# Attention queries and keys in two fp32r parts over 48 rows, two heads per tile at rows 0 and 64

## What is computed

```python
q_half = q_lat @ Wq_up.T + bq_up
q = concatenate([q_half, apply_rotary(q_half, cos, sin)], -1)
k_half = kv_lat @ Wk_up.T + bk_up
k = concatenate([k_half, apply_rotary(k_half, cos, sin)], -1)
v = kv_lat @ Wv_up.T + bv_up
scores = einsum('bhqd,bhkd->bhqk', q, k) / sqrt(16)
out = einsum('bhqk,bhkd->bhqd', softmax(scores), v)
h = out @ Wo.T + bo
```

## Time and profile before

| | us |
|---|---|
| median of 3 runs | 823.37 |
| lowest and highest | 819.76, 823.95 |
| span of the profiled execution | 817.9 |
| start of the first score's maximum | 36.59 |
| end of the last score's maximum | 132.1 |
| start of the output projection's transposes | 150.00 |

### The profile page before, as it was taken

The page is one execution under the profiler, slowest core; times in us unless marked ns, Lnnn a source line. Parts: engine busy times, 40 slices in busy tenths (PEclk is TensorE's granted clock), DMA queues, the critical chain, the costliest instruction groups (busy, mean ns, idle before and its releaser), DMA issues. The chain is left out here.

```text
span 817.9 us, 11514 instructions
## 1 busy us (share of the span) xinstructions
PE 752.8 (92%) x3994; PEld 553.5 (68%) x4004; DVE 541.3 (66%) x1323; ACT 266.5 (33%) x421; POOL 221.1 (27%) x190
## 2 busy tenths in 40 slices
PE   5989999999999999999999498998957999999995
PEld 4422332477888888887456387777743899999995
DVE  4798996467555555555799999999577354334346
ACT  2555678453343434343571111121230100000000
POOL 4542000022232323231030000876002254434321
PEclk9999999999999999999999799999987999999997
DMA  8594000101111111140122405200014999999972
GB/s 297 172 200 94 3 2 2 59 21 38 39 50 46 55 41 54 42 155 1 40 77 81 190 1 171 62 1 1 1 52 154 320 346 346 342 340 347 342 260 97
DMA packets 39333, 101.04 MB, mean 124 GB/s; under 512 B 5374, under 2 KB 19894, under 8 KB 38326
## 3 DMA queue, kind: packets, MB, share of 16 engines
q1 hardware_dynamic: 35334, 91.06, 34.4%
q0 software_dynamic: 3504, 8.98, 2.9%
q10 hardware_dynamic: 448, 0.39, 0.2%
HBM read 84.17 MB, written 16.44 MB: 123 GB/s over the span
## 5 line engine op out<-in xcount | busy, mean ns | idle before, releaser
L1365 PE MATMUL psum<-xr,wr 128*128 128x512 f32 x600 | 145.6, 393 | 1.0 <-DVE arena L2017 1.0
L1365 PEld LDWEIGHTS psum<-xr,wr 128*128 128x128 f32 x600 | 113.6, 190 | 25.3 <-issue 1.7
L735 POOL TENSOR_TENSOR wr<-ring,wr 128x512 fp32r<-128x512 f32 (+1 forms) x50 | 54.9, 1119 | 237.5 <-ACT wr L914 145.9
L1680 PEld LDWEIGHTS psum<-arena 128*128 128x128 f32 x700 | 83.5, 192 | 3.3 <-issue 1.5
L1680 PE MATMUL psum<-arena 128*128 128x128 f32 x700 | 83.9, 275 | 1.1 <-ACT arena L1118 0.6
L1690 PE MATMUL psum<-arena 128*128 128x256 f32 x350 | 81.3, 379 | 0.0
L2480 DVE TENSOR_SCALAR arena<-psum,arena 128x256 f32<-128x256 f32 x35 | 16.9, 484 | 94.1 <-PE psum L1690 94.1
L1376 PE MATMUL psum<-hr,wr 128*128 128x512 f32 x300 | 76.6, 391 | 0.9 <-DVE hr L1954 0.9
L1865 DVE TENSOR_REDUCE small<-psum 128x1 f32<-128x512 f32 x112 | 71.1, 685 | 9.0 <-PE psum L1241 8.3
L1980 DVE TENSOR_TENSOR hid<-hid,psum 128x512 f32<-128x512 f32 x50 | 34.4, 687 | 58.6 <-ACT hid L920 58.4
L889 ACT ACTIVATE arena<-psum 128x1024 f32<-128x1024 f32 x64 | 63.1, 1023 | 27.9 <-PE psum L1251 27.2
(11 more groups left out here) (391 smaller groups left out, 1219.9 us busy)
## 6 DMA issues: line engine op xcount, KB each, us to landing
arena<-in_w1u SPq DMA_DIRECT2D x35, 642.5 KB
arena<-in_w1d SPq DMA_DIRECT2D x35, 640.0 KB
ring<-in_w SPq DMA_DIRECT2D x25, 384.0 KB, 3.1
z_scratch<-w_a SPq DMA_DIRECT2D x4, 768.0 KB, 7.1
arena<-z_scratch SPq DMA_DIRECT2D x8, 384.0 KB, 5.9
arena<-part_scratch SPq DMA_DIRECT2D x9, 256.0 KB, 7.6
qkv_scratch<-arena SPq DMA_DIRECT2D x4, 512.0 KB, 2.7
arena<-qkv_scratch SPq DMA_DIRECT2D x4, 512.0 KB, 4.0
```

The lines of the kernel that those rows point to most:

```text
L735: pool.tensor_tensor(wr0[:, k, LO, part], ring0[:, k, part], wr0[:, k, HI, part], ALU.subtract).then_inc(s["w0_lo"], 1)
L1365: ins = pe.matmul(bank[2 * b + m][:, :], wr0[:, k, w, lo:lo + P], xr[:, x, f, half(b)], start=(f == 0 and (w, x) == PARTS[0]), stop=(f == ...
L1680: ins = pe.matmul(bank[2 + r % 2 * 3 + k // 2][:, tile(k % 2)], wup1[:, r % NW, lo:lo + P], xgT[:, r % 2, f, :], start=(f == 0), stop=(f = ...
```

## The change

- Queries and keys are held in two parts, high and low, as fp32r; three pairings (HI HI, HI LO, LO HI) make 48 rows instead of 96. A row tile holds two heads side by side and two at partition 0 and 64 (`head_rows`); the maxima's rows are 48, 49 and 112, 113.
- For tiles 0 and 2, ACT makes the high part straight from PSUM, DVE the low part in one instruction; for the rotated tiles ACT and POOL do one each. Four writes per pair and batch replace six, of 4-byte words. Rows are loaded in eight issues per tile instead of seven. Rows of ones are filled once and copied by DMA.
- Every group's maxima, the first too, go through DRAM, in two loads for the two row halves. SP's loop over the groups also issues the rows of tiles 2 and 3.
- PE: the value projection comes first, then 28 scores (`FIRST`) ahead of the loop, with the gate rows' chunks, their transposes and warming matmuls between them; in the loop each step alternates `scores_t` of one half with a score of the other, two scores per step throughout. The maxima of a group are transposed four scores after its last.

The diff, cut to its core:

```diff
 HG = 4
 NG = NH // HG * B
 Q = P // HG
-KP = (0, 1, 2, 0, 1, 0)
-QP = (0, 0, 0, 1, 1, 2)
-KRUN = ((0, 3), (3, 5), (5, 6))
-QRUN = ((0, 1), (1, 2), (2, 4), (4, 6))
+HI, LO = 0, 1
+PARTS = ((HI, HI), (HI, LO), (LO, HI))
+KP = (HI, LO, HI)
+QP = (HI, HI, LO)
+KRUN = ((0, 2), (2, 3))
+QRUN = ((0, 1), (1, 3))
 KR = HD * len(KP)
+HROW = P // 2
+HP = HG // 2
 DK, DV = 8, 16
 E0, K0, I0 = 16, 6, 176
...
-AHEAD = 4
-HI, LO = 0, 1
-PARTS = ((HI, HI), (HI, LO), (LO, HI))
+FIRST = HG * TB + 12
+MAX_LAG = 4

...
+        def head_of(n):
+
+            return n // 8 % HP, 1 - n % 2, n // 2 % TB
+
...
+            first = FIRST + 2 * (2 * TB * g + p)
+            return range(first, min(first + 2, NG * HG * TB))
+
+        def maxima_after(n):
+
+            g, over = divmod(n + 1 - MAX_LAG, HG * TB)
+            return g - 1 if over == 0 and g > 0 else None
...
         def k_rows(eng, t, own, name):
-            for r, end in KRUN:
-                eng.dma_start(Kt[t][r * HD:end * HD, :, own], piece_rows(1, t, r, end)[:, :, own])\
-                   .then_inc(s[name], 16)
+            for jb in range(2):
+                for r, end in KRUN:
+                    eng.dma_start(head_rows(Kt[t], jb, r * HD, end * HD)[:, :, own].bitcast(F32),
+                                  piece_rows(1, t, r, end, jb)[:, :, own]).then_inc(s[name], 16)

         def q_rows(eng, t, own, name):
-            for r, end in QRUN:
-                eng.dma_start(Qt[t][r * HD:end * HD, :, own], piece_rows(0, t, r, end)[:, :, own])\
-                   .then_inc(s[name], 16)
+            for jb in range(2):
+                for r, end in QRUN:
+                    eng.dma_start(head_rows(Qt[t], jb, r * HD, end * HD)[:, :, own].bitcast(F32),
+                                  piece_rows(0, t, r, end, jb)[:, :, own]).then_inc(s[name], 16)
+
+        def ones_rows(eng, t, name):
+            for jb in range(2):
+                eng.dma_start(head_rows(Kt[t], jb, KR, KR + 2).bitcast(F32), ones_row).then_inc(s[name], 16)

...
             parts_out(1, 2 * B, slice(0, TOK))
-            sp.wait_ge(s["v_mm"], NT // 2)
-            sp.wait_ge(s["parts_out1"], 16 * 6)
-            all_rows(2)
-
-            for g in range(1, NG):
+            for g in range(NG):
                 sp.wait_ge(s["bank_free"], bank_turn["maxima", g] + 1)
-                if g > 1:
-                    sp.wait_ge(s["max_in"], HG + 16 * (g - 1))
+                if g:
+                    sp.wait_ge(s["max_in"], 32 * g)
                 load("max_out", max_dram, max_sb[:, g % 2, :])
-                sp.wait_ge(s["max_out"], 16 * g)
-                load("max_in", Qt[g // B][KR:KR + 2, :, half(g % B)],
-                     max_dram.rearrange("(h j t) q -> h j (t q)", h=2, j=HG))
-                if g == 1:
-                    all_rows(3)
+                sp.wait_ge(s["max_out"], 16 * (g + 1))
+                for jb in range(2):
+                    load("max_in", head_rows(Qt[g // B], jb, KR, KR + 2)[:, :, half(g % B)].bitcast(F32),
+                         max_dram.rearrange("(h j o t) q -> h o j (t q)", h=2, j=HP, o=2)[:, jb])
+                if g < 2:
+                    if g == 0:
+                        sp.wait_ge(s["v_mm"], NT // 2)
+                        sp.wait_ge(s["parts_out1"], 16 * 4)
+                    all_rows(2 + g)
+                    ones_rows(sp, 2 + g, f"ones_in{2 + g}")
...
             ch = Chain(pool, s["pool"])
-            pool.memset(Ks[KR:KR + 2, :, :, :], 1.0).then_inc(s["ones"], 1)
+            pool.memset(ones_row, 1.0).then_inc(s["ones"], 1)
             pool.wait_ge(s["ones"], 1)
             pool.memset(V[:, :, :, HD:HD + 1], 1.0).then_inc(s["ones"], 1)
             pool.wait_ge(s["ones"], 2)
+            for t in range(2):
+                ones_rows(pool, t, "ones_in")
             pool.dma_start(sel0[:, :], a["sel0"]).then_inc(s["ld_sel0"], 16)
             pool.dma_start(tri[:, :, :], a["tri"]).then_inc(s["ld_sel0"], 16)

             pool.wait_ge(s["ld_cs"], 16)
...
             for b in range(B):
                 for n in range(2):
                     act.wait_ge(s["up"], 2 * b + n + 1)
+                    act.activation(high[:, 2 * n, half(b)].bitcast(F32R), bank[4 * b + 2 * n][:, :], ACT.Identity,
+                                   bias=cols[:, BUP + 2 * n:BUP + 2 * n + 1]).then_inc(s["part1"], 1)
+            for b in range(B):
+                for n in range(2):
+                    act.wait_ge(s["part2"], 2 * b + n + 1)
                     act.activation(X[:, 2 * n, half(b)], bank[4 * b + 2 * n][:, :], ACT.Identity,
                                    bias=cols[:, BUP + 2 * n:BUP + 2 * n + 1]).then_inc(s["up_copy"], 1)
-                for n in range(2):
-                    act.wait_ge(s["up_copy"], 2 * b + n + 1)
-                    first_piece(2 * n, half(b))
-                for n in range(2):
-                    second_piece(2 * n, 2 * b + n + 1, half(b))
-            act.wait_ge(s["parts_out0"], 16 * 6)
-            q_rows(act, 0, half(0), rows_in(0, 0))
-            act.wait_ge(s["part3"], 3)
+                if b == 0:
+                    act.wait_ge(s["parts_out0"], 16 * 4)
+                    q_rows(act, 0, half(0), rows_in(0, 0))
             act.wait_ge(s["mod_mm"], 2)
             for x in range(2):
-                act.activation(mod_rows[:, x, :], bank[1 + 2 * x][:, :], ACT.Copy).then_inc(s["mod_rows"], 1)
+                act.activation(mod_rows[:, x, :], bank[3 + 2 * x][:, :], ACT.Copy).then_inc(s["mod_rows"], 1)
             for n in range(2):
                 act.wait_ge(s["rotated"], 2 * n + 2)
-                first_piece(2 * n + 1, slice(0, TOK))
...
-            for n in range(MODC):
+            for m in range(NT // 2):
+                if m == 0:
+                    pe.wait_ge(s["up_copy"], 2)
+                    pe.wait_ge(s["part2"], 2)
+                if m == 2:
+                    pe.wait_ge(s["up_copy"], 4)
+                    pe.wait_ge(s["part2"], 4)
+                for x in range(2):
+                    ins = pe.matmul(bank[V_BANKS[m]][:, x * D:(x + 1) * D], lat[:, tile(2 * m + x)], wv,
+                                    start=True, stop=True)
+                ins.then_inc(s["v_mm"], 1)
+
+            def modulate_rows(n):
+
                 layer, lo = (0, 2 * D + 512 * n) if n < 2 else (1, 512 * (n - 2))
                 for k in range(KD):
-                    ins = pe.matmul(bank[1 + n // 4 * 2][n % 4 * Q:n % 4 * Q + B, :], ccol[:, layer * KD + k, :],
+                    ins = pe.matmul(bank[3 + n // 4 * 2][n % 4 * Q:n % 4 * Q + B, :], ccol[:, layer * KD + k, :],
                                     wmod[layer][:, k, lo:lo + 512], start=(k == 0), stop=(k == KD - 1))
-            ins.then_inc(s["mod_mm"], 1)
-
-            pe.wait_ge(s["up_copy"], 4)
-            for m in range(NT // 2):
+                if n == MODC - 1:
+                    ins.then_inc(s["mod_mm"], 1)
+
+            def mod_turned():
+                pe.wait_ge(s["mod_rows"], 2)
                 for x in range(2):
-                    ins = pe.matmul(bank[2 * m][:, x * D:(x + 1) * D], lat[:, tile(2 * m + x)], wv,
-                                    start=True, stop=True)
-                ins.then_inc(s["v_mm"], 1)
-
-            pe.wait_ge(s["swapped"], 4)
-            pe.wait_ge(s["mod_rows"], 2)
-            for x in range(2):
-                for n in range(4):
-                    ins = pe.transpose(bank[5 + 2 * x][:, tile(n)], mod_rows[:, x, tile(n)], ident[:, :])
-            ins.then_inc(s["mod_mm"], 1)
-            pe.wait_ge(s["v_in"], NT // 2)
+                    for n in range(4):
+                        ins = pe.transpose(bank[4 + 2 * x][:, tile(n)], mod_rows[:, x, tile(n)], ident[:, :])
+                ins.then_inc(s["mod_mm"], 1)

             def next_bank(*name):
...
             def scores(n):

-                g, j, qt = n // (HG * TB), n // TB % HG, n % TB
+                g, (jj, jb, qt) = n // (HG * TB), head_of(n)
                 b, t = g % B, g // B
                 if n % (HG * TB) == 0:
                     pe.wait_ge(s[rows_in(t, b)], ROWS_IN)
                 to = next_bank("scores", n)
-                pe.matmul(to, Qt[t][0:KR, j, b * S + qt * P:b * S + (qt + 1) * P],
-                          Kt[t][0:KR, j, half(b)], start=True, stop=True).then_inc(s["bank_full"], 1)
-
-            def scores_t(g, kt, pair):
-
-                n, b, t = 8 * g + 2 * kt + pair, g % B, g // B
-                if n >= 2:
+                pe.matmul(to, head_rows(Qt[t], jb, 0, KR)[:, jj, b * S + qt * P:b * S + (qt + 1) * P],
+                          head_rows(Kt[t], jb, 0, KR)[:, jj, half(b)], start=True, stop=True)\
+                    .then_inc(s["bank_full"], 1)
+
+            def scores_t(g, kt, pair, jb):
+
+                n, b, t = 2 * TB * g + 2 * kt + pair, g % B, g // B
+                if n >= 2 and jb == 0:
                     pe.wait_ge(s["exp"], n - 1)
-                for x in range(2):
```

(91 more changed lines are left out.)

157 lines of the change are left out of this document (60 added, 97 removed).

## The result

| | before | after |
|---|---|---|
| time, median (range) of four runs each | 822.36 us (819.76 to 823.95) | 839.91 us (838.84 to 840.45) |
| ratio | 1 | 1.021, interval 1.018 to 1.023 |
| span of the profiled execution, and its own time | 817.9 us, not listed | 836.7 us, 838.84 us |
| transposes behind attention begin | 150.00 us | 166.68 us |
| maximum 47 ends | 71.8 us | 88.7 us |

The kernel became 2% slower; 818 was forecast, with 811 to 828 as the range. Of the 18.8 us between the two spans 16.7 are there when attention ends, and 16.9 already when the third group's maxima end. What is left behind attention (836.7 - 166.68 = 670.0 us against 667.9) is no more than other profiles differ there without any edit behind attention (668.4 to 675.1 us).

What follows compares the result with a forecast made beforehand. PE was taken as the bound in the long stretch, VectorE close behind. Setup 0.5, steady stretch 4.2 and end 0.5 sum to 5.2 us off 823.4, giving 818; range 811 to 828.

Steps and rivals of the forecast that it cites:

- The base: Whole program: span 817.9 us, median 823.37, 5.5 above; a microsecond leaving the span is taken from the median, one for one.
- The setup: Stretch before the loop: first maximum at 32.0 instead of 36.59, that lead spent on separate gate chunks; 0.5 us counted.
- GpSimd's subtractions of 2.1 each come then: Setup, second pair's pieces: after ScalarE's roundings, subtractions end at 50.3 and 52.4, last write issued by 52.9.
- from there VectorE paces: Setup, from maximum 16 at about 49.6: maxima 0.61 us each, maximum 27 ending at 56.9.
- PE idles about two us ahead of the loop: Just before the loop: reason to count 0.5 us, though maximum 47 was put at 70.9 against 71.8 before.
- forecast loop start of 57.8: End of setup: last write issued by 52.9, then write 2.2, two loads 1.3, landing 1.4.
- The steady stretch: 71.9 to 132.1 us: row halves overlap, and of VectorE's 4.63 us idle time 4.2 comes back.
- VectorE with 2.5 sets the pace: Steady cycle: PE needs only 2.0 us with overlapping halves, so VectorE's four maxima at 2.5 set the cycle.
- The end: Last maximum (132.1) to 150.0: shorter score pairs give back part of 3.7 us idle; bounds 0 to 1.0, 0.5 taken.
- Rival 1: First stage: gate chunks overlap their neighbours and cost little, loop at 52.4, time 812.8 us; chance 0.12.
- Rival 2: Steady stretch: the halves don't overlap, cycle 2.91 instead of 2.83, time 824 us; chance 0.14 (half-way form, 820 us, 0.09).
- Rival 3: Three group starts: maxima wait behind row loads in SP's queue, three times 3.65 us, time 829; chance 0.15.

Runs made afterwards that it cites:

- e3: The changed kernel with all five gate chunks ahead of the first score, and one warming matmul per score where the chunks were: 833.76 us, ratio 1.010.
- e1: The changed kernel with the first group's maxima kept in PSUM until split, and the single warming matmuls in banks 4 and 3: 835.51 us, ratio 1.013.
- e4: The changed kernel with ScalarE's copies of the turned query and key halves ahead of its gate-row copies: 835.78 us, ratio 1.013.
- e11: The kernel before with the first group's maxima kept in SBUF instead of PSUM: 822.52 us, ratio 0.999.
- e2: The changed kernel with seven warming matmuls just ahead of the first score: 839.99 us, ratio 1.019.
- e9: e6 with the second pair's writes behind the first maxima, seven warming matmuls before the first score, two per chunkless score from score 20: 829.43 us, ratio 1.008.
- e10: The changed kernel with the value matmuls taking 256 of their 512 columns: 851.46 us, ratio 1.036.
- e5: e4 with two warming matmuls behind each score from score 13 on, where there was one: 836.56 us, ratio 1.018.
- e12: e9 with the third and fourth tiles' row loads issued one group later and two warming matmuls per score in the loop's first three steps: 824.40 us, ratio 1.003.
- e13: e5 with the value matmuls taking 384 of their 512 columns: 834.88 us, ratio 1.010.
- e15: The changed kernel with each value block cut by columns, 256 queries of all four heads behind each score of the step: 842.02 us, ratio 1.025.
- e7: The changed kernel with the head order turned, so a score and the transposed score ahead of it use the same row half: 844.50 us, ratio 1.025.
- e6: e4 with the five gate chunks cut into ten halves, one after every second score: 826.36 us, ratio 1.007.
- e16: e12 with value blocks cut by columns, whole again once no maxima are left, and the fourth tile's row loads in two parts: 821.16 us, ratio 0.9995.
- e8: The changed kernel with each value block split by heads, two matmuls behind each score of the step: 855.99 us, ratio 1.041.

## Why the prediction was wrong

**The base.** after's own profiled execution took 838.84 us with a span of 836.7, so 2.1 us lie around the span. The prediction found 5.5 between before's span and its median; some 3.4 of them mean only that the profiled execution of before was quicker than the median. Taking the saving from the median was sound, and no part of the miss comes from there.

**The setup, first part: sizes.** The first maximum began at 34.28, not 32.0: the first score waited 1.81 us for the query rows' DMA, which the sum had not priced. Rounds at full clock are 2.98 us, not 2.8: from 44.28, score 0.43, warming 0.32 and the next score 0.42 around a chunk of 1.81. Alone the score and the warming matmul would be 0.227 and 0.217, so each passage between 48-row scores and matmuls of 128 rows costs about 0.15 rather than 0.1. The Trainium skill, "TensorEngine Tiling (Array Packing)", Key Properties, has a change of mode drain the engine; the trace is in keeping with that, but the number format changes at these passages as well, and no run parts the two. Chunks apart were costed rightly: 1.81 against 1.76, and e3 shows them at 3.59 us for all five when together.

**The setup, second part: two terms that the sum put at nothing or nearly so.** The steps "GpSimd's subtractions of 2.1 each come then" and "from there VectorE paces" were each priced, but not against one another. VectorE's split of the first maxima reads and writes SBUF at that very time, and waits for GpSimd's instruction to end: 3.0 us (1.10 + 2.27 instead of 0.34). e1 (source in PSUM), e4 (GpSimd earlier) and e11 (the kernel before made to collide) show it from three sides. The Trainium skill, "SBUF — State Buffer", section "SBUF: two separate sides", says that VectorE and GpSimd share a pair of ports which one of them holds for a whole instruction, if VectorE's instruction has two inputs in SBUF or works in a mode that takes both ports. The trace agrees in that each small instruction ends with one of GpSimd's; the second has both inputs in SBUF, the first only one, and its mode is not in the trace. The kernel before had that buffer in PSUM.

The larger term is the clock. The prediction priced every matmul at full speed; for "PE idles about two us ahead of the loop" it took 0.4 us off the 0.9 that it had in hand, and nothing anywhere else. In after PE idles 1.81 us before the first score and has half the clock until 41.5; it idles 1.56 us behind the split, and has half the clock from 62.4 to 82.6. e2 parts the first cause: without that idling the first fall is gone. The second fall needs no idling, since it comes in e3 and e4 with PE busy throughout. What PE did ahead of it was, in after, e2, e3 and e4, scores of 48 rows with one warming matmul each, and in e1 and e9 the loop's first steps, of which three have no value block; the clock came back when value blocks ran, and in e10, with half of their columns, it did not. So thin work is what the falls have in common. That it is the cause is argued and not shown: the same pairs kept the full clock for over ten microseconds in e1, and e5 doesn't decide it. Nor does the kernel before: its sixteen scores of 96 rows in bf16, with one warming matmul each as well (0.60 us a pair), kept a clock of 1.00, but only from 36.17 to 44.75, no longer than the new pairs did in e4. e12, with more warming in both places, kept the full clock through attention in its trace, beside its other edits. What is shown is the price: the new pair takes 0.75 us at full clock, because of the passages, and 1.26 at half.

From the forecast loop start of 57.8 to 71.8 are 14.0 us: 2.3 the first score, 4 the clock (and passages) up to the first chunk's end, 1.2 the later rounds (the first of them partly at half clock), 3 the split, 4 the scores at half clock. The forecast had the loop wait for the maxima's load; in after that load was issued by 65.6, and what held the loop to 71.8 were PE's own scores. The loop's first cycles at half clock put another 4 on top (88.7 - 71.8 = 16.9 to maximum 47, forecast 13.1).

**The steady stretch.** From the third group's last maximum to the last one before took 60.27 us and after 59.84: 0.43 us came where 4.2 were forecast. The assumption in doubt, that the halves overlap, was right. The step that failed is "VectorE with 2.5 sets the pace". VectorE needs 2.48, and then waits 0.2 for a score: three banks hold three scores, the fourth (96.16) must wait until VectorE has freed one, and only behind it does PE do a value block of 1 us and a score that is ready 0.5 us after it starts; meanwhile VectorE has three maxima, 1.9 us. e13 shortens the block, e15 cuts it, and they get 11.26 and 11.47 us a group; the forecast's 11.0 to 11.4 was the price without that wait. PE went from busy throughout to 56.74 of 59.9 us, and VectorE has 54.88 of them: neither is full, the bound is the loop through both.

**The end.** 18.1 us from the last maximum, against 17.9; the 0.5 did not come.

**The rivals.** Rival 1 (chunks hidden) fell: the maxima came in pairs 2.98 us apart. Rival 2 (no overlap) fell, by the starts at 94.87 and 94.88; its price was not tested, since e7 keeps the overlap. Rival 3 (maxima behind row loads) does not show in after: its row loads were issued from 65.76 to 85.8, and the loads of the first three groups' maxima 1.4 us after their writes. It was hidden by the setup's lateness: as soon as e6 and e9 moved the loop forward such a wait cost 3.5 and 4.2 us of standing PE, beside half the clock. One later write in after, issued at 127.40 with no row load near it, took 3.55 us and made its group 12.27 us long; before has two such, 3.3 us at 86.85 and 3.1 at 110.97. Why was not found.

**What stays open.** e16 removes what was found and is level with before, 3 us above the forecast of 818. In its trace the loop starts at 56.1, earlier than the forecast's 57.8, but from maximum 47 to the last one it takes 58.6 us, so that 1.65 of the 4.2 us came: undisturbed groups are 11.48 us, and the two with late loads cost 0.46 and 0.75 more. The rest wasn't parted. What lets the clock fall in one execution of a kernel and not in another wasn't found either.

## What to carry over

Price an edit that makes matmuls smaller in the clock as well as in their time: look at what the engine does in each stretch once the work is thinner, and at every idle microsecond ahead of it. Two engines' instructions that a reorder brings together in time must be checked for what they share, and a producer and a consumer joined by few buffers have a pace of their own, slower than either engine's work alone would set. Work that lies side by side in the array is only cheap as a whole: moved apart or cut the wrong way it costs its full time in each place.

## What the runs showed of the hardware

- The granted clock fell to half with PE shown busy without a gap (e4, 1.00 of 1.00 us in each of 60 to 61 and 61 to 62). In e10 it stayed at half for 48 us of unbroken matmuls, from 92 to 140.
- Matmuls over opposite row halves start together (94.87 and 94.88 in after), and one whose half is free starts ahead of an earlier one whose half is taken (e7, 116.78 and 117.12).
- VectorE's 128x16 cast from SBUF took 1.10 (after) and 1.80 us (e11) beside GpSimd's subtraction and 0.17 when it read PSUM (e1) or GpSimd was idle (e4).
- Two value matmuls take 1.04 us, four 1.05 (e8); four over half the columns 0.63 (e15), over 384 columns 0.84 (e13).
- A passage between matmuls of 48 rows in fp32r and of 128 in bf16 costs PE about 0.15 us each way (a pair 0.75 us); between 96 rows and 128, both in bf16, before's trace shows none (score and warming matmul in turn, 0.22 us apart from 36.17 on).
- A write of 16 KB in a quiet queue mostly landed 1.4 us after its issue, once 3.55 (127.40 in after); it landed after 6.4 us behind four writes of 512 KB (e6) and after 6.7 behind another tile's row loads (e9).
